# Transformer blocks on one core: first MLP products issued two tiles ahead, the last projection set between MLP steps, key loads set ahead of head saves

## The chip, the cores and the metric

The kernel runs on one core of a Trainium2 chip. The metric is the device time of one execution in microseconds; the kernel before has a median of 2254.26 us over 3 runs (2253.84 to 2258.37). Lower is better.

## The reference

```python
# x [8, 100, 512], ctx [8, 361, 512], float32
def L0(x):                       # 16 heads of width 128, keys extended by a bias row
    x = x + cross_attention(layer_norm(x), ctx, wq1, ..., bias_k1, bias_v1)
    x = x + cross_attention(layer_norm(x), ctx, wq2, ..., bias_k2, bias_v2)
    h = layer_norm(x)
    return x + gelu(h @ w_fc1 + b_fc1) @ w_fc2 + b_fc2          # 512 -> 2048 -> 512
def L1(x):                       # 16 heads of width 32
    q, k, v = layer_norm(x) @ q_w + q_b, ctx @ k_w + k_b, ctx @ v_w + v_b
    out = softmax(where(mask, q k^T / sqrt(32), min)) v
    x = x + out @ cproj_w + cproj_b
    y = gelu_tanh(layer_norm(x) @ fc_w + fc_b)
    return x + y @ proj_w + proj_b                              # 512 -> 2048 -> 512
out = L1(L0(x))
```

## The kernel before

**Layout.** Activations lie transposed: 128 features on the partitions, 400 rows (four batches of 100) along the free axis, in two halves; x is `xT[:, half, c]` with four chunks c of features. Every product of full precision is made of three matmuls on a high and a low part of each operand (`split_mms`), so one 128x512 weight tile against one half is 12 matmuls of 400 columns. The high part is a ScalarE copy with rounding, the low part a VectorE subtraction; for weights GpSimd makes both (`split`: L757 and L759).

**Order.** Nothing is scheduled at run time. Each engine has its own program with semaphore waits. Weight tiles come in one list, `JOBS`, sorted by a due step; SP loads them in that order into three stage buffers (`load_jobs(jobs_due(step) + 3)`), GpSimd splits them in that order into a ring of four slots (`mring`; a few go into `w1`), and a slot is free when the product that read the tile four places earlier has ended. SP's queue also carries context loads, saves and loads through DRAM, and issues strictly in its order: a wait in front of one item holds all behind it.

**Stages.** Two large attention blocks (up to step 256, not touched), MLP 0, the small attention, MLP 1. An MLP has 32 steps F, 16 for each half of the rows. `up(f)` multiplies weight tile ("a", f) with the normed input into a bank (bank f % 2); `gelu_high(f)` applies gelu into `gtmp` and rounds it into `part`; `gelu_low(f)` makes the low part; `down(f)` multiplies tile ("b", f) with the part tile into four accumulating banks `ACC`. TensorE runs `up(F+1)`, `down(F)` in step F. `up(16)` reads the norm of the second half. After 16 steps `mlp_add` adds the four banks to x on VectorE. `MLP_NORM` says in which step of an MLP a layer norm starts: norm 5 in step 0 and norm 6 in step 16 of MLP 0, norm 9 in step 0 of MLP 1. A norm started at step F takes sum at F+1, mean at F+2, centring and squares at F+3, their sum at F+4, variance at F+5, root and reciprocal at F+6, four scales on VectorE (L1548) and four high parts on ScalarE at F+7, four low parts on VectorE (L1495) at F+8. In each step VectorE does its gelu tile first.

**Between.** `queries1(0..3)` makes the queries of half 0 (query 0 in the last MLP step, in banks 0 and 1 by turns), SP saves them to DRAM (`save_q`) and loads them rearranged (`load_q`); then `keys1` in bank 0 and `values1` in banks 5, 6, 1 for the first batch. The high part of query Q >= 2 waits for the save of query Q - 2.

**Small attention.** 32 steps s of four units: logits (L1095), softmax, three transposes (L1106), `value_sums1` two steps behind. In each step SP saves the heads of step s - 3 (`save_heads`, L626, waits for the low part of the value sum), loads the keys of step s + 1 (`load_k`, L621, three issues), saves keys (L611), loads queries once in four steps (L605) and the heads back (`load_heads`, L636, four issues). `project1(0, c)` is done in step 19. At the end TensorE does the last two value sums, `up(32)` in step 32, `up(33)`, `up(34)`, then waits for the last heads, does `project1(1, c)` for the four c into banks 5, 6, 2, 3, and starts MLP 1 with `down(32)` behind the additions to x (L1505).

## Time and profile before

| | |
|---|---|
| median of 3 runs | 2254.26 us |
| profiled execution, its own time | 2260.57 us |
| its span, first to last instruction | 2258.8 us |
| mean granted TensorE clock | 0.987 |
| TensorE matmul busy | 2161.1 us (96%) |
| VectorE busy | 1605.4 us (71%) |
| ScalarE busy | 1183.9 us (52%) |
| GpSimd busy | 943.8 us (42%) |
| DMA, 16 engines | 52.5% on the hardware queue |

Busy is the time in which the engine executes an instruction; its idle time costs only where another engine waits for what comes late. The granted clock is 1 at 2.4 GHz; a stretch with a lower mean has spent a part of its time at 1.2 GHz. Times in rows count from the start of the span.

### The profile page before, as it was taken

To read this page: it belongs to the slowest core of one execution; us is meant where nothing else is said; L and a number is where in the kernel's file an instruction comes from. 1 tells how busy PE (TensorE), PEld (TensorE's weight loads), DVE (VectorE), ACT (ScalarE), POOL (GpSimd) and SP (SyncE) were. 2 spreads that over 40 slices of the span, in tenths; PEclk is the share of its full clock that TensorE was granted. 3 is DMA by queue.
4 is the path that set the end of the run, shared out by engine and by line. 5 is a ranking of instruction groups with operands and counts; after the bars stand their busy time and mean duration, and the time that the engine had idled before them with its cause. 6 is when DMAs were issued, how large, how long until landed. Compare 5 with 4: busy or idle time off the path is not lost.

```text
span 2258.8 us, 36858 instructions
## 1 busy us (share of the span) xinstructions
PE 2161.1 (96%) x12468; PEld 2099.6 (93%) x12468; DVE 1605.4 (71%) x3635; ACT 1183.9 (52%) x2838; POOL 943.8 (42%) x898
## 2 busy tenths in 40 slices
PE   6999999999999999999999999999999899998899
PEld 5999999999999999999999999998899778887899
DVE  6777688777778877777887777777466487788353
ACT  4555465555555555555555555565243376667232
POOL 4314444241444424234342424432788332232597
PEclk9999999999999999999999999999999999998999
DMA  4646455554645555464555546454543667765243
GB/s 136 140 87 142 102 121 101 120 128 83 151 101 113 102 125 122 85 148 105 110 110 116 126 83 151 109 102 83 139 125 103 167 189 199 206 199 160 84 132 108
DMA packets 162454, 283.08 MB, mean 125 GB/s; under 512 B 35424, under 2 KB 92896, under 8 KB 162272
## 3 DMA queue, kind: packets, MB, share of 16 engines
q1 hardware_dynamic: 162272, 280.73, 52.5%
q8 instruction: 105, 1.72, 0.3%
q14 instruction: 77, 0.63, 0.1%
HBM read 237.66 MB, written 29.88 MB: 118 GB/s over the span
## 4 chain that ended last, share of the span: by engine, by line
PE 80%; DVE 6%; DMA 4%; ACT 3%; POOL 3%; issue 2%; SPq 2%; POOLq 0%; DVEq 0%; ACTq 0%
PE bank L838 76%; PE bank L926 3%; POOL mring L759 1%; DMA ctxN_raw<-in_ctx 1%; POOL mring L757 1%; DVE ln_c L1548 1%; DVE hT L1495 1%; SPq L636 1%; DVE lnb L1541 1%; PE bank L1106 1%; ACT prob L1340 1%; DMA k<-k_parts 1%; DVE prob L1662 1%; POOL ln_c L813 1%; DMA y_parts<-qs 0%
## 5 line engine op out<-in xcount | busy, mean ns | idle before, releaser
L838 PE MATMUL bank<-ctxT,kring 128*128 128x362 f32 x3456 | 629.6, 330 | 4.4 <-DVE qs L1495 2.7
L757 POOL TENSOR_SCALAR mring<-stage 128x512 fp32r<-128x512 f32 x325 | 233.3, 718 | 899.2 <-PE bank L838 734.2
L838 PEld LDWEIGHTS bank<-ctxT,kring 128*128 128x128 f32 x3456 | 587.2, 190 | 7.6 <-issue 4.7
L838 PE MATMUL bank<-pT,ctxN 128*128 128x400 f32 (+1 forms) x2304 | 470.0, 351 | 0.6 <-DVE U L1499 0.3
L759 POOL TENSOR_TENSOR mring<-stage,mring 128x512 fp32r<-128x512 f32 x325 | 444.9, 1369 | 27.1
L838 PEld LDWEIGHTS bank<-pT,ctxN 128*128 128x128 f32 (+1 forms) x2304 | 407.1, 188 | 2.4 <-issue 1.2
L838 PE MATMUL bank<-hT,mring 128*128 128x400 f32 x1608 | 320.0, 348 | 13.8 <-DVE hT L1495 10.5
L838 PEld LDWEIGHTS bank<-hT,mring 128*128 128x128 f32 x1608 | 296.1, 190 | 18.3 <-issue 15.0
L838 PE MATMUL bank<-U,mring 128*128 128x400 f32 x1536 | 303.3, 348 | 8.1 <-issue 6.3
L838 PEld LDWEIGHTS bank<-U,mring 128*128 128x128 f32 x1536 | 275.3, 188 | 10.3 <-issue 7.9
L1234 ACT ACTIVATE kT<-bank,cols 128x361 fp32r<-128x361 f32 (+1 forms) x288 | 160.8, 558 | 211.8 <-PE bank L838 211.7
L1499 DVE TENSOR_TENSOR ctxN<-ctxN_raw,ctxN 128x384 fp32r<-128x384 f32 x256 | 189.2, 742 | 81.9 <-ACT ctxN L1234 81.9
L1234 ACT ACTIVATE U<-bank 128x400 fp32r<-128x400 f32 x256 | 127.8, 499 | 146.2 <-PE bank L838 144.3
L1499 DVE TENSOR_TENSOR U<-bank,U 128x400 fp32r<-128x400 f32 x256 | 146.2, 571 | 74.8 <-ACT U L1234 73.8
L1577 DVE TENSOR_SCALAR_CACHE_REDUCE prob<-bank 100x362 f32<-100x362 f32 x256 | 135.1, 528 | 88.1 <-PE bank L838 88.0
L1282 ACT ACTIVATE prob<-prob,stat 100x362 f32<-100x362 f32 x256 | 151.1, 590 | 74.7 <-DVE prob L1577 74.7
L1234 ACT ACTIVATE pT<-bank 128x300 fp32r<-128x300 f32 x384 | 160.0, 417 | 54.0 <-PE bank L926 37.6
L1499 DVE TENSOR_TENSOR pT<-bank,pT 128x300 fp32r<-128x300 f32 x384 | 175.6, 457 | 5.8 <-ACT pT L1234 5.8
L1234 ACT ACTIVATE ctxN<-ctxN_raw 128x384 fp32r<-128x384 f32 x256 | 131.7, 516 | 85.3 <-DMA ctxN_raw<-in_ctx 85.2
L838 PE MATMUL bank<-kT,qT 128*100 128x362 f32 x768 | 169.2, 328 | 4.2 <-DVE kT L1495 4.2
L1499 DVE TENSOR_TENSOR part<-gtmp,part 128x400 fp32r<-128x400 f32 x64 | 75.3, 1178 | 136.6 <-ACT part L1234 136.3
L1495 DVE SCALAR_TENSOR_TENSOR kT<-bank,cols,kT 128x361 fp32r<-128x361 f32 (+1 forms) x288 | 168.2, 584 | 4.6 <-ACT kT L1234 4.6
(103 smaller groups left out, 2942.1 us busy)
## 6 DMA issues: line engine op xcount, KB each, us to landing
ctxT_raw<-in_ctx SPq DMA_DIRECT2D x72, 724.0 KB, 7.5
ctxN_raw<-in_ctx SPq DMA_DIRECT2D x256, 192.0 KB, 3.6
k<-k_parts SPq DMA_DIRECT2D x96, 181.0 KB, 3.7
stage<-in_wk SPq DMA_DIRECT2D x64, 256.0 KB, 4.1
stage<-in_wq SPq DMA_DIRECT2D x64, 256.0 KB, 4.5
stage<-in_wv SPq DMA_DIRECT2D x64, 256.0 KB, 4.0
stage<-in_wo SPq DMA_DIRECT2D x64, 256.0 KB, 2.7
stage<-in_fa SPq DMA_DIRECT2D x64, 256.0 KB, 2.6
```

Of the source, the lines that this page charges most:

```text
L636: sp.dma_start(f32(attnT[r, :, a:a + LQ]), y_dram[t, r, :, i * LQ:(i + 1) * LQ]).then_inc(S.at_in, 16)
L757: nc.gpsimd.tensor_scalar(hi, src, 1.0, 1.0, ALU.mult, ALU.mult).then_inc(S.w_hi, 1)
L759: nc.gpsimd.tensor_tensor(lo, src, f32(hi), ALU.subtract).then_inc(S.w_ready, 1)
L813: nc.gpsimd.tensor_tensor(y, y, lnb[:, 1, :], ALU.mult).then_inc(S.ln_y, 1)
L838: mm = pe.matmul(dst, parts_l[a], parts_r[b], start=first and k == 0, stop=last and k == len(order) - 1)
L926: mm = pe.transpose(bank[T_BANK][:, t * LQ:(t + 1) * LQ], prob[0:LQ, n % PB, t * P:(t + 1) * P], ident[0:LQ, 0:LQ])
L1106: mm = pe.transpose(bank[T1_BANK[u % 2]][:, t * LQ:(t + 1) * LQ], prob1[0:LQ, u % PB, t * P:(t + 1) * P], ident[0:LQ, 0:LQ])
L1234: return nc.scalar.activation(dst, src, ACT.Identity, bias=bias)
L1282: nc.scalar.activation(x, x, ACT.Exp, scale=-1.0, bias=nmax[0:LQ, k:k + 1], accum_out=denom[0:LQ, k:k + 1]).then_inc(S.exp_ready, 1)
L1495: return nc.vector.scalar_tensor_tensor(out=dst, in0=src, scalar=bias, in1=f32(hi), op0=ALU.add, op1=ALU.subtract)
L1499: return nc.vector.tensor_tensor(dst, src, f32(hi), ALU.subtract)
L1577: nc.vector.tensor_scalar(prob[0:LQ, k, 0:LT], bank[2 + n % 2][0:LQ, 0:LT], -SCALE0, None, ALU.mult, ALU.min, accum_out=nmax[0:LQ, k:k + 1 ...
```

## The change

- `up(F + 2)` is issued in step F instead of `up(F + 1)`, on three banks (`UP_BANK`) with three part and gelu buffers (`MB = 3`). The list of tiles gives `a(f + 2)` ahead of `b(f)`.
- Query 0 is made in step 30 and query 1 in step 31 of MLP 0; the queries use banks 6, 0, 1, 6. `keys1(0)` waits for two queries instead of three, `values1(0, 1)` for four, `values1(0, 2)` for three.
- `up(32)` and `up(33)` are issued inside the attention's steps 32 and 33, behind the first third of a value sum. `project1(1, c)` is done behind `down` in steps 2 to 5 of MLP 1, all in bank 6, each waiting for the addition before; `down(32)` no longer waits for it.
- Norm 9 starts in step 5 of MLP 1 instead of step 0.
- In SP's loop `load_k` stands ahead of `save_heads`.

```diff
+MB = 3
-MLP_NORM = {0: {0: 5, 16: 6}, 1: {0: 9}}
+MLP_NORM = {0: {0: 5, 16: 6}, 1: {5: 9}}
...
         if f + 2 <= NF - 1:
-            add(T_MLP[0] + f - 1, "b", f)
-            add(T_MLP[0] + f, "a", f + 2)
-        else:
-            add(T_MLP[0] + f - 1, "b", f)
+            add(T_MLP[0] + f - 1, "a", f + 2)
+        add(T_MLP[0] + f - 1, "b", f)
     for j in range(4):
-        add(T_MLP[0] + NF - 1 + j // 2, "1q", j)
+        add(T_MLP[0] + NF - 2 + j // 2, "1q", j)
...
     for f in range(1, NF):
+        if f + 2 < NF:
+            add(T_MLP[1] + f - 1, "a", F + f + 2)
         add(T_MLP[1] + f - 1, "b", F + f)
-        if f + 2 < NF:
-            add(T_MLP[1] + f, "a", F + f + 2)
...
+        UP_BANK = [[0, 1, 6], [0, 1, 5]]
...
-        CPROJ_BANK = [[1, 1, 1, 1], [5, 6, 2, 3]]
+        CPROJ_BANK = [1, 6]
+        F_CPROJ = 2
...
         def q1_bank(Q):
-            return bank[Q % 2 if Q < 4 else X1_BANK][:, 0:ROWS]
+            return bank[[6, 0, 1, 6][Q] if Q < 4 else X1_BANK][:, 0:ROWS]
...
             for s in range(NS + BEHIND):                         # SP
+                if s + 1 < NS:
+                    load_k(s + 1)
                 if s >= BEHIND + 1:
                     save_heads(s - BEHIND - 1)
-                if s + 1 < NS:
-                    load_k(s + 1)
...
                 for F in range(NF):                              # TensorE
-                    if 1 <= F < NF - 1 and (m == 0 or F > 1):
-                        up(NF * m + F + 1)
-                    elif F == NF - 1 and m == 0:
-                        queries1(0)
+                    if F + 2 < NF:
+                        up(NF * m + F + 2)
+                    elif m == 0:
+                        queries1(F + 2 - NF)
                     down(NF * m + F)
+                    if m == 1 and F - F_CPROJ in range(DC):
+                        project1(1, F - F_CPROJ)
...
+                    if s >= NS and i == 0:
+                        up(NF + s - NS)
...
-                if s == NS:
-                    up(NF)
-            up(NF + 1)
-            up(NF + 2)
-            for c in range(DC):
-                project1(1, c)
             mlp_steps(1)
...
                 for F in range(NF):                              # VectorE; ScalarE alike
-                    if 1 <= F < NF - 1:
-                        gelu_low(NF * m + F + 1)
-                    elif F and m == 0:
-                        query1_low(0)
+                    if F + 2 < NF:
+                        gelu_low(NF * m + F + 2)
+                    elif m == 0:
+                        query1_low(F + 2 - NF)
+                    if m == 1 and F - F_CPROJ in range(DC):
+                        projected1(1, F - F_CPROJ)
```

## Rows read from the trace of the kernel before

**Rows 1.** Stretches: us; busy of PE, PEld, DVE, ACT, POOL; clock, DMA share, GB/s

```profile
1612.00:1765.00 153.00, 144.29 (x761) 140.82 (x762) 91.63 (x88) 56.37 (x95) 138.80 (x130) 0.98 0.43 131
1765.00:1793.00 28.00, 23.43 (x113) 20.90 (x111) 7.81 (x13) 6.48 (x10) 5.04 (x5) 0.94 0.73 178
...
2089.00:2118.00 29.00, 20.73 (x95) 19.74 (x95) 5.76 (x9) 4.63 (x7) 3.83 (x4) 0.86 0.23 77
2118.00:2256.00 138.00, 134.94 (x736) 133.02 (x735) 61.29 (x58) 41.49 (x71) 119.63 (x116) 1.00 0.37 112
```

**Rows 2.** Chain that ended last, merged: start us, us, what

```profile
2190.07 63.99 PE bank L838 x351
```

**Rows 3.** Timeline of TensorE, first MLP: start, us, line, count, idle before and releaser

```profile
1611.98 2.41 PE L838 MATMUL bank<-part,w 128*128 128x400 f32 x12 [0.76 <-DVE xT L1504]
...
1653.47 2.41 PE L838 MATMUL bank<-part,mring 128*128 128x400 f32 x12 [0.67 <-DVE part L1499]
...
1659.99 3.98 PE L838 MATMUL bank<-part,mring 128*128 128x400 f32 x12 [1.93 <-DVE part L1499]
...
1734.95 2.40 PE L838 MATMUL bank<-part,mring 128*128 128x400 f32 x12 [1.32 <-DVE part L1499]
...
1740.45 2.42 PE L838 MATMUL bank<-part,mring 128*128 128x400 f32 x12 [0.92 <-DVE part L1499]
```

**Rows 4.** Groups by line, 1612 to 1765: busy us, mean ns | idle before

```profile
L759 POOL TENSOR_TENSOR mring<-stage,mring 128x512 fp32r<-128x512 f32 x63 | 89.4, 1419 | 5.3
...
L757 POOL TENSOR_SCALAR mring<-stage 128x512 fp32r<-128x512 f32 x63 | 48.7, 773 | 14.4 <-PE bank L838 12.5 <-DMA stage<-in_fb 1.5
```

**Rows 5.** Timeline, from the MLP to the first logits

```profile
1768.30 9.32 SPq L594 DMA_DIRECT2D q_parts<-qs  x8
...
1775.04 3.11 PE L838 MATMUL bank<-ctxT,kring 128*128 128x362 f32 x12 [2.74 <-DVE qs L1495]
...
1775.43 0.59 ACT L1234 ACTIVATE qs<-bank,cols 128x400 fp32r<-128x400 f32 x1 [1.20 <-DMA q_parts<-qs]
...
1793.04 0.54 PE L1095 MATMUL bank<-k,q 96*100 96x362 f32 x1 [1.87 <-DMA k<-k_parts]
```

**Rows 6.** Waits of TensorE, 1793 to 2089: us, times, longest

```profile
PE bank L1095 <- DMA k<-k_parts: 9.2, 3, 4.5
...
PE bank L1095 <- issue: 2.2, 3, 1.2
```

**Rows 7.** Timelines of SP and of TensorE at the longest of these waits

```profile
2001.13 0.43 SPq L626 DMA_DIRECT2D y_parts<-qs  x1
...
2007.80 0.41 PE L1095 MATMUL bank<-k,q 96*100 96x362 f32 x1 [4.50 <-DMA k<-k_parts]
```

**Rows 8.** Timeline behind the small attention, into the second MLP

```profile
2089.01 2.87 PE L838 MATMUL bank<-hT,mring 128*128 128x400 f32 x12
...
2101.39 2.45 SPq L636 DMA_DIRECT2D qT<-y_parts  x4
...
2105.46 11.36 PE L838 MATMUL bank<-qT,w 128*128 128x400 f32 x48 [6.59 <-DMA qT<-y_parts]
...
2117.75 4.59 PE L838 MATMUL bank<-part,mring 128*128 128x400 f32 x24 [0.93 <-DVE xT L1505]
```

**Rows 9.** Timeline of the second MLP, steps 7 to 10

```profile
2145.31 2.35 PE L838 MATMUL bank<-hT,mring 128*128 128x400 f32 x12
...
2149.60 5.05 DVE L1548 SCALAR_TENSOR_TENSOR ln_c<-ln_c,cols,lnb 128x400 f32<-128x400 f32 x4
...
2156.90 5.05 DVE L1495 SCALAR_TENSOR_TENSOR hT<-ln_c,cols,hT 128x400 fp32r<-128x400 f32 x4
...
2157.13 2.40 PE L838 MATMUL bank<-part,mring 128*128 128x400 f32 x12 [0.74 <-DVE part L1499]
...
2162.99 2.42 PE L838 MATMUL bank<-part,mring 128*128 128x400 f32 x12 [1.28 <-ACT part L1234]
```

**Rows 10.** Timeline of VectorE inside the attention, GpSimd idle: the lows of norm 8

```profile
2077.96 1.17 DVE L1495 SCALAR_TENSOR_TENSOR hT<-ln_c,cols,hT 128x400 fp32r<-128x400 f32 x2
```

More of the change, by code:

```diff
@@ L1001, in up @@
                 for c in range(DC):
-                    mm = split_mms(bank[f % 2][:, 0:ROWS], w_cols(key, c), [hT_c(hT, 0, c), hT_c(hT, 1, c)],
+                    mm = split_mms(up_bank(f), w_cols(key, c), [hT_c(hT, 0, c), hT_c(hT, 1, c)],
                                    c == 0, c == DC - 1)
@@ L1019, in down @@
                 for c in range(DC):
-                    mm = split_mms(bank[ACC[c]][:, 0:ROWS], w_cols(key, c),
-                                   [part[f // NF][:, f % 2, p_, :] for p_ in range(2)],
+                    mm = split_mms(bank[ACC[c]][:, 0:ROWS], w_cols(key, c), gelu_parts(f),
                                    f % FF == 0, f % FF == FF - 1)
@@ L1133, in project1 @@
                         pe.wait_ge(S.q1_lo, 8)
[L1134 to L1135 removed]
+                    else:
+                        pe.wait_ge(S.y_lo, NS)
+                else:
+                    pe.wait_ge(S.c_add, DC * half + c)
                 for j in range(4):
[L1137 removed]
+                    mm = split_mms(bank[CPROJ_BANK[half]][:, 0:ROWS], w_cols(("1c", half, j), c),
                                    [attnT[:, p_, j * ROWS:(j + 1) * ROWS] for p_ in range(2)], j == 0, j == 3)
@@ L1185, in _ @@
             mlp_steps(0)
-            for Q in range(1, 4):
+            for Q in (2, 3):
                 queries1(Q)
@@ L1301, in gelu_high @@
                     act.wait_ge(S.a_mm, NS - 4)
-                if f >= 2:
-                    act.wait_ge(S.m_lo, f - 1)
-                    act.wait_ge(S.dn_mm, f - 1)
-                g = gtmp[f // NF][:, f % 2, :]
-                nc.scalar.activation(g, bank[f % 2][:, 0:ROWS], gelu, bias=col_c(bias, f % FF))\
+                if f % NF >= MB:
+                    act.wait_ge(S.m_lo, f - MB + 1)
+                    act.wait_ge(S.dn_mm, f - MB + 1)
+                g = gelu_out(f)
+                nc.scalar.activation(g, up_bank(f), gelu, bias=col_c(bias, f % FF))\
                     .then_inc(S.m_gelu, 1)
                 act.wait_ge(S.m_gelu, f + 1)
-                high(part[f // NF][:, f % 2, 0, :], g).then_inc(S.m_hi, 1)
+                high(gelu_parts(f)[0], g).then_inc(S.m_hi, 1)
             def query1_high(Q):
@@ L1438, in _ @@
             mlp_steps(0)
-            for Q in range(1, 4):
+            for Q in (2, 3):
                 query1_high(Q)
@@ L1698, in projected1 @@
                 dve.wait_ge(S.c_mm, DC * half + c + 1)
-                add_to_x(half, c, bank[CPROJ_BANK[half][c]][:, 0:ROWS], "L1_xattn_cproj_b").then_inc(S.c_add, 1)
+                add_to_x(half, c, bank[CPROJ_BANK[half]][:, 0:ROWS], "L1_xattn_cproj_b").then_inc(S.c_add, 1)
             def context_low(i, k):
@@ L1818, in _ @@
             mlp_steps(0)
-            for Q in range(1, 4):
+            for Q in (2, 3):
                 query1_low(Q)
@@ L1862, in _ @@
                     norm_low(8, (2 * (t - 10), 2 * (t - 10) + 1))
-                if s == NS:
-                    gelu_low(NF)
-            gelu_low(NF + 1)
-            for c in range(DC):
-                projected1(1, c)
+                if s >= NS:
+                    gelu_low(NF + s - NS)
             mlp_steps(1)
```

60 lines of the change are left out of this document (32 added, 28 removed).

## The prediction

> **What bounds the kernel now.** I read the busy time by stretch first [rows 1]. TensorE is the busiest engine in every stretch, and the change can only touch the last 650 us. Its idle time there is small and lies in known places: 8.7 us in the first MLP (153.00 - 144.29), 4.6 between MLP and attention, 8.3 of 29 behind the attention, 3.1 in the second MLP. The clock column shows where it also runs at the lower of its two levels, 1.2 instead of 2.4 GHz, for a part of the time: 0.94 ahead of the attention, 0.86 behind it. GpSimd, which splits each weight tile, is busy 138.80 of 153.00 us in the first MLP and 119.63 of 138.00 in the second. So TensorE sets the end, and GpSimd stands close behind it.
>
> Next, what one unit of work costs. The chain of waits has 351 matmuls in 63.99 us without a gap, 0.182 each, so a group of 12 (an `up`, a `down` or a `project1`) takes 2.19 us at the full clock [rows 2]. All sums below are in such groups.
>
> **First MLP.** TensorE's rows with a wait in front [rows 3] give the gaps of one kind: the VectorE half of a gelu tile comes late. 0.67 and 1.93 us behind norm 5, 1.32 and 0.92 behind norm 6. Behind the second, 12 matmuls took 3.98 us where the group behind the first took 2.41: the clock had fallen, 1.6 us more. The reader is to see that VectorE works off the four scales and four lows of a norm, some ten microseconds, around two gelu tiles. The change lets `up` run one step (two groups, 4.4 us) further ahead, with a third bank and a third part buffer, so between the end of `up(F)` and `down(F)` lie four groups, not two. All four gaps are shorter than the 4.4 us won, so I count them all as gone, with the clock they cost: 0.67 + 1.93 + 1.6 + 1.32 + 0.92 = 6.4. At the MLP's start `down(0)` waited 0.76 for the residual sum; `up(2)` now stands ahead of it and needs only an earlier sum: 0.8 more. The wait for x in front of `down(16)` stays: `mlp_add` still follows the end of `down(15)` on VectorE, behind one gelu tile and one weight tile, and one `up` covers 2.2 us of that, as before.
>
> What could take this back is GpSimd. It does a tile in 0.773 + 1.419 = 2.19 us on average [rows 4], as long as TensorE's group. Its 14.2 idle us of the stretch are partly given by TensorE's own gaps. Taking 7.2 out of the stretch leaves it 7.0, so the tiles still arrive, narrowly. Term: -7.2; bounds 0 (GpSimd takes over, every gap becomes a wait for a tile) and -7.2.
>
> **Between the MLP and the attention.** SP could start saving the queries only at 1768.30, behind a weight load that waits for the split of the last query tile, and that split waits for `down(31)`. The high part of query 2 waits for that save's landing, that of query 3 for the next one's, until 1775.43, and TensorE waited 2.74 for query 2's bank, until 1775.04; its next 12 matmuls took 3.1 us, partly at the lower clock [rows 5]. The change runs query 1 before `down(31)`: the split, and with it SP, comes one group (2.2 us) later against the work done, and query 3's low about 2.2 later. But `keys1(0)` now needs the banks of queries 0 and 1 only, and runs with `values1(0,0)` under the wait; what waits for query 3 is `values1(0,1)`. Behind query 2's low TensorE did one keys (3.1 us), two values and a second keys, and on that one hang the split, the save and the load of the keys, up to the first logits at 1793.04. Now the second keys hangs on query 3's low instead, with one values ahead of it; query 3's low ends at 1776.1 (high and low are 0.6 each), 1.1 behind 1775.04. So a keys and a values fall out of the chain, 3.1 and about 2.7 (12 x 0.182 x 512/400), and 1.1 comes in: 4.7 less; minus the 2.2 that SP starts later, minus some matmuls at the lower clock behind the wait: about -2. Bounds 0 and -4.6 (the stretch's whole idle time).
>
> **Keys first in SP's queue.** At each step `load_k` (three DMA issues) went behind `save_heads`, which waits for the value sum. Key loads came late three times, 9.2 us in all, 1.87 of it at the first logits; the two others make 7.3. Three more gaps in front of logits, 2.2 us, have no releaser shown [rows 6]. At the longest one, until 2007.80, SP came late out of its weight loads and issued the save (0.43 us) at 2001.13, then the keys [rows 7]; without the save in front they go half a microsecond earlier and are not behind its bytes. I take the small gaps for those at the first logits of a batch, where the query load stands behind `load_k`: with the keys issued during the wait for the value sum, it goes earlier by three issues, which at SP's 0.43 to 0.6 us for one covers them (1.2 the longest). What queues behind `load_k` now is `save_heads`; where the logits of the step before aren't done, it goes up to 1.5 us later, and ScalarE needs its landing only a step later. The Trainium skill (DMA: Bandwidth & Descriptors, Queues, rings and completion order) says that an engine takes descriptors in ring order; it speaks for the same direction and gives no price. I take -3: 2 for the small gaps, 1 for the two of half a microsecond. Bounds 0 and -9.5 (7.3 + 2.2).
>
> **Behind the attention.** The last heads come back by loads issued from 2101.39 to 2103.84, and TensorE stands 6.59 us until 2105.46 [rows 8]. Then the four `project1` take 11.36 us for 48 matmuls, where 48 x 0.182 is 8.7: 2.6 for the clock. `down(32)` waits 0.93 more. Lost in all: 10.1. In the new order TensorE has work between the end of `up(32)` (2091.9) and the heads, 13.6 us later: `up` 33 to 36 and `down` 32 to 34, seven groups of 2.19, are 15.3 us, and the last value sums come on top. The heads are there first. Against this: `up(32)` moves ahead of the second value sum, into a stretch at the lower clock (it took 2.87 there where 2.19 is full rate, and would take up to 4.0): 1.1, and it shifts the last head output by about 0.6, which is covered. And the tile of `down(34)` is loaded only behind the head loads in SP's queue, from 2103.8 on (0.6 later with the shift). With some 2.5 us to landing (between the 1.6 of the last head load and the 4.1 of the first) and 2.2 to split it is ready near 2109.4, where TensorE, behind its fifteen microseconds and the value sums, wants it at 2108 to 2109: I count 0.9. SP's order of the weight loads follows TensorE's new order. Term: -10.1 + 1.1 + 0.9 = -8.1. Bounds -5.5 (the clock falls all the same) and -10.1. The four additions to x lie on VectorE in steps that are a group longer than before.
>
> **Norm 9 in the second MLP: the new wait.** The norm of the second half moves from step 0 to step 5, since x is complete only after `project1`. Its low part then lies in step 13, and `up(48)`, which reads it, is issued in step 14; before, the low stood in step 8 and the product in step 15. [Rows 9] have the same sequence, five steps earlier: the `up` of the scaling step starts at 2145.31; the four scales end at 2154.65; ScalarE's high parts hold up the next gelu; the four lows run 2156.90 to 2161.95, 16.6 us after that start. TensorE reaches `up(48)` four groups after it, 8.7 us. So it waits 7.9 us, if VectorE's rows stay as long. They won't quite: with TensorE standing, GpSimd fills its four slots and stops, and the same low step took 1.17 for two, 0.59 each, when GpSimd was idle [rows 10], instead of 1.26. That takes 2.5 off: 5.4. I take 6.5. After such a wait the clock falls: 1.6 us were lost behind 1.93 of waiting [rows 3], 2.6 behind 6.59 [rows 8]; I take 2.0. What is given back is what norm 9 cost before, 0.74 and 1.28 [rows 9]. Term: +6.5 + 2.0 - 2.0 = +6.5. Bounds +3.4 (5.4, no fall) and +8.5 (7.9 and 2.6).
>
> The Trainium skill has a rule for each part. GPSIMD Engine Reference, Architecture: GpSimd's physical read and write port is shared with VectorE; the trace agrees (0.59 against 1.26), and by it the wait is nearer to 5.4. TensorE: Matmul & The Clock Gate, HAM oscillation, tells how an idle gap drops the clock and the work behind it is paid at half rate; it speaks against any new wait, so the sum would be nearer to +8.5.
>
> **Sum.** -7.2 - 2 - 3 - 8.1 + 6.5 = -13.8. The profiled execution took 2260.57 us (span 2258.8 and 1.8 around it) and goes to 2246.8. It lies 6.3 above the median of the three runs, 2254.26; I carry the difference over to that: 2240.5.
>
> **Rivals.**
> 1. GpSimd takes over in the first MLP (7.2 of gain gone): 2240.5 + 7.2 = 2247.7. For it: 2.19 against 2.19. Against: four slots of lead and 7.0 us left. Chance 0.14.
> 2. The new wait costs its upper bound and the keys gain nothing: 2240.5 + 2.0 + 3 = 2245.5. For it: a clock that fell after each gap. Chance 0.15.
> 3. The keys come early enough to empty both late loads and norm 9 meets an idle GpSimd: -9.5 instead of -3, +3.4 instead of +6.5: 2230.9. For it: the longest wait, 4.50, came right behind the save. Against: SP was late by more than the save. Chance 0.12.
> 4. No change that can be told: the upper bounds of norm 9, keys and the tail together with half of GpSimd's: 2240.5 + 2 + 3 + 2.6 + 3.6 = 2251.7. Chance 0.06.
> 5. Slower: after the wait at `up(48)` the clock stays at the lower level. 34 groups follow, each 2.19 us longer at 1.2 GHz. From 6.3 such groups on (13.8 / 2.19) the gain is gone, from 8.4 on it is slower by more than 0.2%; with 16, half of them, it is 2240.5 + 35.0 = 2275.5. Against it: the longest fall behind a wait that the rows show costs 2.6 us. Chance 0.05.
>
> The forecast itself keeps 0.48, with 2236 to 2245 as its own range. Two tenths of a per cent, 4.5 us, is about what a measurement of this kernel can tell from no change: 2249.8 and below is faster. That holds for the forecast, rivals 1 to 3 and a part of 4: 0.88; same 0.07, slower 0.05. The range 2232 to 2249 holds the forecast, rivals 1 and 2 and half of rival 3.
>
> **What would show it.** In the trace after: no wait of TensorE for a gelu part in the first MLP, and its stretch some 7 us shorter; no wait for the head loads, and no fall of the clock around it; one wait of 5 to 8 us in front of the 12 matmuls of `up(48)`, released by VectorE's low (hT, L1495 of before), with 3 to 5 us of matmuls longer than 2.35 behind it; waits on the key loads of 6 us instead of 7.3 and none of the small ones. I am wrong if GpSimd's tiles are named as releaser all through the MLPs, if `values1(0,1)` waits more than 3 us, or if the wait at `up(48)` is not there.

## The result

The changed kernel is slower by 0.6%. Beside four runs of the kernel before (median 2255.42 us, 2253.84 to 2258.37) four runs of it gave a median of 2269.42 us (2265.68 to 2274.33); the ratio is 1.0062, with a 95% interval of 1.0039 to 1.0084. The interval is clear of 1, so the sign is sure. I had forecast 2240.5, range 2232 to 2249. The profiled execution took 2274.33 us, span 2272.5, clock 0.983. Lines of the changed code stand 9 or 10 further down than those named above (`split_mms` is L848, logits L1105, `save_heads` L636, `load_heads` L646, `load_k` L631; L627 is the place in `load_k` where SP waits for the logits of the step two before, which free the key buffer).

### The profile page after: what moved, and what is told of

It is laid out like the page before. It is cut to its first block, busy times and chain, and to the rows that moved or that the text cites. A ratio compares the mean times of both kernels' runs of the same rounds, so it can differ in the third digit from the quotient of the medians.

```text
span 2272.5 us, 36855 instructions
## 1 busy us (share of the span) xinstructions
PE 2170.3 (96%) x12468; PEld 2106.2 (93%) x12468; DVE 1594.9 (70%) x3635; ACT 1182.5 (52%) x2838; POOL 943.1 (42%) x898
## 4 chain that ended last, share of the span: by engine, by line
PE 79%; DMA 6%; POOL 5%; DVE 3%; SPq 3%; ACT 2%; issue 2%; POOLq 0%; DVEq 0%; ACTq 0%
PE bank L848 74%; POOL mring L769 3%; PE bank L936 3%; DMA y_parts<-qs 3%; POOL mring L767 2%; SPq L646 2%; DMA ctxN_raw<-in_ctx 1%; SPq L631 1%; PE bank L1116 1%; DMA stage<-in_fb 1%; DVE hT L1504 1%; POOL ln_c L823 1%; PE bank L1105 0%; ACT prob L1350 0%; DVE ln_c L1557 0%
## 5 line engine op out<-in xcount | busy, mean ns | idle before, releaser
L848 PE MATMUL bank<-ctxT,kring 128*128 128x362 f32 x3456 | 630.3, 330 | 1.1 <-DVE ctxT L1508 1.1
L848 PEld LDWEIGHTS bank<-ctxT,kring 128*128 128x128 f32 x3456 | 588.7, 190 | 3.4 <-issue 1.4
L848 PE MATMUL bank<-pT,ctxN 128*128 128x400 f32 (+1 forms) x2304 | 471.1, 352 | 0.0
L848 PEld LDWEIGHTS bank<-pT,ctxN 128*128 128x128 f32 (+1 forms) x2304 | 408.7, 189 | 1.4 <-issue 0.2
L848 PE MATMUL bank<-hT,mring 128*128 128x400 f32 x1608 | 326.7, 353 | 24.9 <-DVE hT L1504 16.0
L848 PEld LDWEIGHTS bank<-hT,mring 128*128 128x128 f32 x1608 | 300.7, 193 | 31.3 <-issue 20.8
L848 PE MATMUL bank<-U,mring 128*128 128x400 f32 x1536 | 304.8, 349 | 8.1 <-issue 6.3
L848 PEld LDWEIGHTS bank<-U,mring 128*128 128x128 f32 x1536 | 276.9, 189 | 10.3 <-issue 7.9
L1244 ACT ACTIVATE pT<-bank 128x300 fp32r<-128x300 f32 x384 | 159.7, 416 | 57.3 <-PE bank L936 37.7
L848 PE MATMUL bank<-kT,qT 128*100 128x362 f32 x768 | 169.2, 328 | 4.2 <-DVE kT L1504 4.2
```

What stands on the lines that cost most here:

```text
L848: mm = pe.matmul(dst, parts_l[a], parts_r[b], start=first and k == 0, stop=last and k == len(order) - 1)
L1244: return nc.scalar.activation(dst, src, ACT.Identity, bias=bias)
```

## The profile after

Busy time by stretch, columns as in [rows 1], cut at the same points of the work:

```profile
1614.00:1768.00 154.00, 145.48 (x770) 140.37 (x769) 91.50 (x88) 56.26 (x95) 141.29 (x130) 0.99 0.43 130
1768.00:1797.40 29.40, 21.95 (x112) 19.20 (x111) 7.74 (x13) 6.33 (x10) 5.56 (x6) 0.95 0.68 168
1797.40:2095.00 297.60, 263.14 (x1479) 230.72 (x1480) 226.16 (x707) 198.38 (x525) 76.26 (x75) 0.95 0.65 186
2095.00:2130.00 35.00, 29.72 (x135) 28.54 (x134) 7.71 (x16) 10.02 (x20) 16.62 (x18) 0.81 0.40 121
2130.00:2270.00 140.00, 132.95 (x713) 131.37 (x712) 60.02 (x59) 38.04 (x65) 105.35 (x105) 0.98 0.35 104
```

No stretch is shorter by what I had promised. Measured from landmark to landmark (first matmul of a stage to first of the next, after minus before, one trace of each, us): up to the last product of the second large attention +2.6 (code that the change doesn't touch), first MLP +0.4, from the third query to the first logits +1.3, attention up to the last batch's value sums +6.8, the tail with the four `project1` -3.4, the second MLP +5.9. That is +13.6 of the 13.8 between the two spans.

**First MLP.** TensorE, rows with a wait in front, as in [rows 3]:

```profile
1678.77 2.46 PE L848 MATMUL bank<-hT,mring 128*128 128x400 f32 x12 [0.56 <-POOL mring L769]
1681.91 2.46 PE L848 MATMUL bank<-part,mring 128*128 128x400 f32 x12 [0.68 <-POOL mring L769]
...
1745.67 2.46 PE L848 MATMUL bank<-hT,mring 128*128 128x400 f32 x12 [0.95 <-POOL mring L769]
...
1760.22 3.95 PE L848 MATMUL bank<-hT,mring 128*128 128x400 f32 x12 [4.02 <-POOL mring L769]
```

The waits for a gelu part are gone; in their place stand waits with GpSimd as releaser, 7.1 us in five places. The longest is for the tile of query 0: in the list it stands behind two tiles, those of `down(30)` and `down(31)`, that TensorE now uses after it. GpSimd's two groups, as in [rows 4], show the same 63 tiles, with 18.2 us idle in front of them instead of 19.7:

```profile
L769 POOL TENSOR_TENSOR mring<-stage,mring 128x512 fp32r<-128x512 f32 x63 | 88.6, 1406 | 5.3
L767 POOL TENSOR_SCALAR mring<-stage 128x512 fp32r<-128x512 f32 x63 | 52.5, 833 | 12.9 <-PE bank L848 11.6 <-DMA stage<-in_fb 1.2
```

**Up to the first logits**, as in [rows 5]:

```profile
1781.26 3.04 PE L848 MATMUL bank<-w,ctxT 128*128 128x512 f32 x12 [1.09 <-DVE qs L1504]
...
1784.58 2.71 SPq L615 DMA_DIRECT2D q<-q_parts  x6
...
1787.34 0.90 SPq L621 DMA_DIRECT2D k_parts<-kT  x2
...
1792.93 2.69 SPq L631 DMA_DIRECT2D k<-k_parts  x6
...
1797.39 0.62 PE L1105 MATMUL bank<-k,q 96*100 96x362 f32 x1 [6.33 <-DMA k<-k_parts]
```

TensorE waits only 1.09 for the queries, as foreseen. But the first key save goes out at 1787.34, behind six query loads, though its low part had ended at 1781.70; 5.6 us after the issue it has landed and the key load may go. The gap moved from the wait for query 2 (2.74 in [rows 5]) to the first logits (1.87 there, 6.33 here).

**Attention.** SP's waits by releaser from 1800 to 2080 (us in total, times, longest), after and then before:

```profile
SPq L646 <- DMA y_parts<-qs: 60.2, 24, 4.0
SPq L627 <- PE bank L1105: 22.1, 11, 6.1
```

```profile
SPq L626 <- DVE qs L1495: 73.1, 23, 6.6
...
SPq L636 <- DMA y_parts<-qs: 7.0, 13, 1.9
```

Before, SP waited for VectorE (the low part of the value sum), that is, it was ahead of the work. After, it waits 24 times for the landing of a head save that it has itself just issued. For TensorE this means, in batches 4 and 5, waits of 1.62 and 5.53 us for key loads and one of 1.87 us for the heads of `project1(0)`; before, its waits for key loads there were 2.85 and 4.50, and it didn't wait for heads. One turn of its queue, after and before:

```profile
2037.73 1.47 SPq L631 DMA_DIRECT2D k<-k_parts  x3
2039.25 0.44 SPq L636 DMA_DIRECT2D y_parts<-qs  x1
2039.73 0.43 SPq L621 DMA_DIRECT2D k_parts<-kT  x1
2043.38 2.45 SPq L646 DMA_DIRECT2D qT<-y_parts  x4
2045.93 1.48 SPq L631 DMA_DIRECT2D k<-k_parts  x3
```

```profile
2033.35 0.34 SPq L626 DMA_DIRECT2D y_parts<-qs  x1
2033.79 1.40 SPq L621 DMA_DIRECT2D k<-k_parts  x3
2035.24 0.43 SPq L611 DMA_DIRECT2D k_parts<-kT  x1
2036.12 2.46 SPq L636 DMA_DIRECT2D qT<-y_parts  x4
...
2044.15 0.34 SPq L626 DMA_DIRECT2D y_parts<-qs  x1
```

Before, three key issues and a key save cover the landing; the turn is 5.2 us and SP idles until the next. After, 3.2 us of the landing are bare, the turn is 8.2 us, and it is followed by the next one at once.

**Tail and norm 9**, timeline as in [rows 8] and [rows 9]:

```profile
2097.04 4.20 PE L848 MATMUL bank<-hT,mring 128*128 128x400 f32 x12
...
2117.69 0.58 SPq L568 DMA_DIRECT2D stage<-in_fb  x1
...
2122.87 4.37 PE L848 MATMUL bank<-part,mring 128*128 128x400 f32 x12 [3.25 <-POOL mring L769]
...
2127.04 3.14 PE L848 MATMUL bank<-qT,w 128*128 128x400 f32 x12
...
2182.34 5.04 DVE L1557 SCALAR_TENSOR_TENSOR ln_c<-ln_c,cols,lnb 128x400 f32<-128x400 f32 x4
...
2189.61 2.27 DVE L1504 SCALAR_TENSOR_TENSOR hT<-ln_c,cols,hT 128x400 fp32r<-128x400 f32 x4
...
2192.02 4.34 PE L848 MATMUL bank<-hT,mring 128*128 128x400 f32 x12 [5.95 <-DVE hT L1504]
2196.16 2.74 PE L848 MATMUL bank<-part,mring 128*128 128x400 f32 x12
```

The wait for heads is gone. Tile b34, loaded behind the last heads at 2117.69, made TensorE wait 3.25 and the clock fell behind it. The new wait in front of `up(48)` is there: 5.95 us, then 2.4 us more for two groups (rows of 4.34 and 2.74, where neighbouring groups at the full clock have rows of 2.35 and 2.33, which overlap by 0.16).

## The experiments

Each run was timed in five rounds (e7 and e7b in three) beside the kernel before; the runs were made on four chips, so the ratios, each against the kernel before on the same chip, compare better than the medians where two runs come from different groups (e1, e2, e3, e6; e4, e7, e7b, e8; e9, e10, e11, e13; e14, e15, e16). Two stretches are read in all traces. A: from the start of the last 39 matmuls of the second attention block's projection to the end of query 3. B: from the first logits of a batch to those of the next, here for batches 4 and 5 (steps 16 to 23).

| kernel | median us | ratio to before | A | first logits wait | batch 4 | batch 5 |
|---|---|---|---|---|---|---|
| before | 2255.42 | 1 | 168.5 | 1.87 | 45.4 | 37.4 |
| after | 2269.42 | 1.0062 (1.0039 to 1.0084) | 168.9 | 6.33 | 49.3 | 44.2 |
| e1: after, heads first | 2259.51 | 1.0014 (1.0000 to 1.0028) | 167.5 | 6.47 | 44.1 | 38.4 |
| e2: before, keys first | 2269.39 | 1.0052 (1.0037 to 1.0067) | 163.5 | 2.22 | 49.8 | 44.6 |
| e3: e1, queries behind `down` | 2255.41 | 0.9995 (0.9984 to 1.0005) | 163.4 | 7.23 | 45.1 | 37.4 |
| e6: after, heads loaded later | 2273.15 | 1.0066 (1.0050 to 1.0081) | 168.4 | 7.05 | 50.0 | 40.4 |
| e8: after, both landings covered | 2268.62 | 1.0059 (1.0044 to 1.0074) | 169.3 | 7.59 | 49.3 | 39.9 |
| e14: after, heads loaded by GpSimd | 2259.72 | 1.0012 (0.9999 to 1.0025) | 167.9 | 6.99 | 45.3 | 37.3 |
| e16: after, weight loads spread | 2271.71 | 1.0062 (1.0049 to 1.0075) | 169.3 | 6.70 | 49.3 | 39.1 |
| e4: e3, norm 9 a step earlier | 2250.39 | 0.9980 (0.9968 to 0.9991) | 162.9 | 6.18 | 42.2 | 37.4 |
| e7: e1, light split | 2244.04 | 0.9945 (0.9929 to 0.9961) | 156.1 | 6.84 | 44.8 | 37.3 |
| e7b: before, light split | 2244.21 | 0.9945 (0.9929 to 0.9960) | 155.5 | 3.72 | 41.7 | 38.4 |
| e9: e4, norm 9 another step | 2247.87 | 0.9960 (0.9944 to 0.9976) | 162.9 | 7.42 | 44.7 | 38.1 |
| e10: e9, first keys ahead | 2242.42 | 0.9935 (0.9921 to 0.9950) | 163.6 | 0.84 | 44.2 | 37.5 |
| e11: e10, weight loads spread | 2237.24 | 0.9913 (0.9899 to 0.9927) | 165.9 | 1.92 | 42.6 | 33.1 |
| e13: e10, high parts on ScalarE | 2237.10 | 0.9910 (0.9896 to 0.9924) | 159.7 | 1.16 | 44.2 | 37.9 |
| e15: e11 and e13 | 2236.87 | 0.9903 (0.9887 to 0.9919) | 159.6 | 0.68 | 45.1 | 33.4 |

### Keys first

**e1, the order of before in SP's queue; e2, that one edit alone on the kernel before.**

```diff
-                if s + 1 < NS:
-                    load_k(s + 1)
                 if s >= BEHIND + 1:
                     save_heads(s - BEHIND - 1)
+                if s + 1 < NS:
+                    load_k(s + 1)
```

> The kernel after with one edit undone: in SP's loop save_heads stands ahead of load_k again. Theory A: with the keys first, the landing of each head save (about 3.3 us) is waited for with nothing issued meanwhile, so SP's turn (8.2 to 9 us) is longer than a step of the attention, and key loads and head loads come late. Then the stretch from the first logits to the turn goes back from 282.3 to about 275.5 us, the head loads at the end come some 2.7 us earlier, and the time is about 2259.5 us, 10 less than after. Theory B: the order is worth what I had priced (-3), and the attention's loss comes from elsewhere, from the phase in which the weight loads meet the key loads, or from up(32) and up(33) inside the last steps. Then the stretch keeps over 280 us and the time is 2270 to 2273.

> The kernel before with one edit of the change: load_k ahead of save_heads. Theory A: slower by 7 to 10 us (2262 to 2265), with SP at work back to back from the middle of the attention, its turn at 8 us or more, and no wait of SP for the low part of the value sums. Theory B, the term as I had predicted it: 2252, 3 less than before, bounds 0 and -9.5.

Theory A held in both, in e1 with its number; e2 cost more than its 7 to 10. e1 is 9.9 us below after (0.0048 in the ratios), e2 is 12.5 above the kernel before of its chip (2256.88). Batches 4 and 5 carry it: 93.5 and 94.5 us with the keys first (after, e2), 82.8 and 82.4 with the heads first (before, e1). My term of -3 was wrong in sign. Without it the rest of the change is worth nothing either (e1 1.0014).

**e6 and e8, keys first, with the landings covered by another order.**

```diff
                 if s + 1 < NS:
                     load_k(s + 1)
+                if s + AHEAD - 1 < NS:              # e8; in e6 the key save stays last
+                    save_k(s + AHEAD - 1)
+                if s >= BEHIND + 2:
+                    load_heads(s - BEHIND - 2)
                 if s >= BEHIND + 1:
                     save_heads(s - BEHIND - 1)
```

> The kernel after, keys first as there, but the heads of a step are loaded one step later, ahead of the next head save, so that no load stands right behind the save that it waits for. Theory A (the unhidden landing is the cost): SP's turn falls by about 3 us, from 8.2 to 9 to about 5.5, the attention's stretch goes from 282.3 to 276 or less; project1(0) in step 19 may wait for heads that come a step later, up to 4 us with its clock. Time 2260 to 2266. Theory B (the order of keys and heads itself, or bytes on the queues, is the cost): the stretch stays over 280 us and the time within 2 us of 2269.4.

> The kernel after with keys first, and SP's turn reordered: load_k(s+1), save_k(s+2), load_heads(s-4), save_heads(s-3). In e6 I had covered the landing of the head save and laid bare that of the key save (load_k followed 3.2 us behind its own save_k). Now each save has issues behind it for the length of its landing. Theory A: a turn is the sum of SP's issues (4.8 us) plus each landing that nothing covers; it falls from 8.2 to 9 to about 5.2, SP waits for the engines again, the stretch from first logits to the turn goes from 282.3 to 274 to 277, and the time to 2259 to 2263. Theory B: keys first costs by itself; the stretch stays over 280 and the time over 2267.

Theory A missed in both, and by its numbers e8 is theory B's (2268.62, the attention as long as in after). In e6 `load_k` stood right behind the key save that it reads, and SP waited for that landing instead, 12.5 us in nine turns: I had uncovered the other of the two landings. In e8 SP's issues of a turn take 4.9 us. In both SP waits for the work again; e6 and then e8, 1800 to 2080:

```profile
SPq L627 <- PE bank L1106: 90.5, 25, 11.7
```

```profile
SPq L627 <- PE bank L1106: 99.4, 26, 12.7
```

So SP was no longer full, and still nothing was won. Batch 5 went from 44.2 to 40.4 and 39.9, but batch 4 stayed at 50.0 and 49.3. The heads, loaded a step later, held `project1(0)` in step 19 for 3.12 and 3.08 us (1.87 in after), and new waits of 3.0 and 3.1 us stand in front of the first logits of batch 4, with no releaser shown. So neither is a clean test of the mechanism. Two readings were left: the landing wait in the queue, or the head save that stands behind `load_k`'s wait for free key buffers.

**e14, the head loads of steps 0 to 29 issued by GpSimd; e16, after with the loads of four weight tiles spread.**

```diff
-                if s >= BEHIND + 1:
+                if s - BEHIND - 1 >= 30:            # SP keeps the last two
                     load_heads(s - BEHIND - 1)
...
+            extra += [(T_ATT1 + t + BEHIND + 1.1, 4, heads_load, t) for t in range(30)]   # GpSimd
```

> The kernel after, keys first, and the head loads of steps 0 to 29 issued by GpSimd, not by SP; only the last two stay on SP. SP then never waits for the landing of a head save, and its turn is three key issues and two saves, about 2.8 us. Theory A (the keys cost because, with them first, nothing lies between a save and the load of the same heads in SP's queue, and all that follows stands behind that landing): batches 4 and 5 (steps 16 to 23) take 80 to 83 us from logits to logits, as in the kernels with heads first, not 93.5; the attention 285 to 290 us, not 296; the time 2258 to 2262. Theory B: with the keys first, load_k's own wait for free key buffers holds the head save (e8: 26 waits, 99 us), ScalarE's value sums and the heads come late whoever loads them; batches 4 and 5 stay over 88 us and the time over 2264.

> The kernel after, keys first, with one edit: the due steps of a32, a33, b32 and a34 spread over four steps, which in e11 took 5 us off the kernel with heads first (batch 5: 37.5 to 33.1 us). Theory A (SP is full: its turn of 8.2 us is as long as a step of TensorE): the spreading can't remove the debt, batches 4 and 5 stay at 88 us or more and after gains under 5 us. Theory B (the keys-first order only lengthens the one stretch in which SP comes late out of the weight loads): batches 4 and 5 fall to 80 or below, and the time to 2259 or below.

e14 decides between these two: 2259.72, the level of e1, with keys first and batches 4 and 5 at 82.6. SP's waits:

```profile
SPq L629 <- PE bank L1119: 136.3, 27, 11.0
```

The head save still stands behind `load_k`'s wait, longer than in e8, and it costs nothing that shows. From the first to the last logits the nine traces with heads first and the weight loads not spread take 284.3 to 290.6 us, the five with keys first and the heads loaded by SP (after, e2, e6, e8, e16) 295.9 to 302.4, and e14 287.1: the two groups don't meet. What costs, then, is the head load in SP's queue once the keys go first. e14 took the landing waits and the four issues (2.5 us) off SP together. The issues alone do no harm where the heads go first (before and e1 have them all, and SP waits for VectorE), and in after the bare landing is what makes the turn too long. But no run takes the landing alone away without a new wait, so its share by itself is argued, not measured. e14 and e1 are level, so keys first shows no gain once the harm is taken away, unless issuing on GpSimd hides one. e16 says little: batch 5 fell by 5.1 us (4.4 from e10 to e11), and theory A's bound for batches 4 and 5 (88) is met by 0.4; batches 2 and 6 came out 3.0 and 2.6 longer in its trace, and the time didn't fall.

### The first MLP

**e3, on e1: the queries behind `down` in the last two steps, in the order of the list of tiles.**

```diff
                     if F + 2 < NF:
                         up(NF * m + F + 2)
-                    elif m == 0:
-                        queries1(F + 2 - NF)
                     down(NF * m + F)
+                    if F + 2 >= NF and m == 0:
+                        queries1(F + 2 - NF)
```

> The kernel of e1 (heads first), and in the last two steps of MLP 0 TensorE does down(F) ahead of the query, as the list of tiles has them. Theory A: the wait of 4.02 us for the tile of query 0 and the clock's fall behind it (1.6 us) are there because that tile is split fourth behind a and b tiles while TensorE asks for it third; in the list's order both go, and the time is 5.6 us below that of e1. Theory B: GpSimd is late here in any order (it had idled under 1 us in the four steps ahead), so the wait only moves to down(30) or down(31), and the time is within 1.5 us of e1's.

4.1 us below e1, stretch A 4.1 shorter: between the two theories. The wait for query 0's tile fell from 4.00 to 1.87, without a fall of the clock behind it: part order, part GpSimd's rate.

```profile
1758.50 2.48 PE L848 MATMUL bank<-hT,mring 128*128 128x400 f32 x12 [1.87 <-POOL mring L769]
```

The six traces with the queries ahead and a full split (after, e1, e6, e8, e14, e16) have A at 167.5 to 169.3, the five with `down` ahead and GpSimd's full split (e3, e4, e9, e10, e11) at 162.9 to 165.9; e11 is the longest because in its trace the clock fell behind the same wait of 1.87.

**e7 on e1, e7b on the kernel before: a light split.** Both leave out three quarters of the low parts of MLP 0's weights and of the first queries.

```diff
+                if key not in IN_W1 and (key[0] in ("a", "b") and key[1] < NF or key[0] == "1q"):
+                    lo, src, hi = lo[:, 0:D // 4], src[:, 0:D // 4], hi[:, 0:D // 4]
                 nc.gpsimd.tensor_tensor(lo, src, f32(hi), ALU.subtract).then_inc(S.w_ready, 1)
```

> The kernel of e1, and in MLP 0 GpSimd makes the low part of a weight tile on 128 of its 512 columns only (the other columns of the low part hold older values: this leaves out three quarters of the low parts of MLP 0's weights and of the first queries, so the output isn't the reference's). GpSimd's 2.19 us for a tile fall to about 1.2. Theory A: GpSimd's rate is what took the place of the gelu waits; the seven waits for tiles (8.8 us, 1.6 for the clock behind the longest) go, the stretch from down(0) to the third query falls from 161.5 to 151 us or below. Theory B: the tiles come late because of the slots of mring and the order of the list; then the longest wait, for query 0's tile, keeps over 2 us and the stretch stays over 156.

> The kernel before with the same edit: the low part of MLP 0's weight tiles on 128 of 512 columns only (three quarters of them left out, the output isn't the reference's). It is the measure for e7: what one tile ahead costs when GpSimd is no limit. Theory A: the waits for gelu parts (4.8 us, 1.6 for the clock) stay for the larger part, since VectorE's norm work around them stays, and are some tenths shorter each as it meets GpSimd less often: the stretch goes from 161.1 to 155 to 158 us, 4 to 7 above e7's. Theory B: GpSimd's share of VectorE's time made these waits too; then they fall under 1 us in all and the stretch equals e7's within 1.5 us, so that two tiles ahead is worth nothing in either case.

For e7 theory A held: no wait for a tile is left, A is 156.1, or 148.7 in the measure of the expectation (less 7.4 for the 39 matmuls). For e7b theory B did: no wait for a gelu part is left and with one tile ahead A is 155.5. So two tiles ahead show no gain with a fast GpSimd. With the full split they show none either: A is 162.9 to 165.9 at best, and 168.5 and 163.5 in the two traces with one tile ahead (before, e2). The gelu lows on VectorE say why; before, and e7b:

```profile
L1499 DVE TENSOR_TENSOR part<-gtmp,part 128x400 fp32r<-128x400 f32 x30 | 34.2, 1142 | 54.8 <-ACT part L1234 54.6
```

```profile
L1501 DVE TENSOR_TENSOR part<-gtmp,part 128x400 fp32r<-128x400 f32 x30 | 17.7, 591 | 75.2 <-ACT part L1236 75.2
```

The same instruction takes 1142 ns beside GpSimd's full split and 591 beside the light one. The gelu parts came late in [rows 3] because of GpSimd's work (e7b changes nothing else), and lookahead turned that debt into late tiles. The Trainium skill (GPSIMD Engine Reference, 1. Specifications) names this case: the interface to SBUF is shared with VectorE and contended by VectorE's instructions with two SBUF inputs. The trace agrees (1142 against 591 ns); gelu part and buffer are two.

**e13, on e10: ScalarE makes the high part of 96 weight tiles of the two MLPs.** The steps in which it works on a norm are left out.

```diff
+            def tile_high(key):                      # ScalarE
+                j = JOB[key]
+                act.wait_ge(S.w_in[j % STAGE], 16 * (j // STAGE + 1))
+                act.wait_ge(*released(IN_M[M_AT[key] - MS]))
+                high(place_of(key)[0], stage[:, j % STAGE, :]).then_inc(S.wa_hi, 1)
...
+                    # step F: tile_high of b(F + 1) ahead of gelu(F + 2), of a(F + 4) behind it
```

> The kernel of e10, and in both MLPs ScalarE makes the high part of most weight tiles (a copy with rounding, as for the value and key weights), GpSimd only the low part: 1.42 instead of 2.19 us for a tile. Skipped in the steps in which ScalarE has a norm's squares, root or high parts. Theory A (from e7 and e7b: GpSimd's time for a tile is what bounds MLP 0, as tiles that come late, and through VectorE's gelu lows, 1.03 to 1.15 us each beside 0.59 with a light split): the waits for tiles in MLP 0 fall from 4 to 8 us to under 2, the stretch by 5 to 8 us, the time 5 to 10 below e10. Theory B: ScalarE's copies, about 0.65 us each and two in a step of 4.4 us, come in front of the gelu of the next tile, and the gelu parts become late instead: no faster than e10, waits named by ScalarE's part.

5.3 us below e10; the waits for tiles fell to one of 1.19, the gelu lows to 824 ns:

```profile
L783 POOL TENSOR_TENSOR mring<-stage,mring 128x512 fp32r<-128x512 f32 x64 | 90.4, 1421 | 36.5 <-ACT mring L1258 31.3 <-PE bank L862 3.4
...
L1532 DVE TENSOR_TENSOR part<-gtmp,part 128x400 fp32r<-128x400 f32 x30 | 24.6, 824 | 55.4 <-ACT part L1258 55.3
```

The time is at the low end of theory A; stretch A is 3.9 shorter, less than its 5 to 8, and GpSimd still makes 19 of the 64 high parts there.

### Norm 9, the first keys, the weight loads

**e4, on e3: project1 and norm 9 one step earlier. e9: norm 9 another step, and b34 loaded ahead of the last heads.**

```diff
-MLP_NORM = {0: {0: 5, 16: 6}, 1: {5: 9}}
+MLP_NORM = {0: {0: 5, 16: 6}, 1: {3: 9}}          # e4: {4: 9}
-        F_CPROJ = 2
+        F_CPROJ = 1
...
             save_heads(NS - 1)
+            load_jobs(JOB[("b", NF + 2)] + 1)         # e9 only
             load_heads(NS - 1)
```

> The kernel of e3 (heads first in SP's queue, queries behind down), with project1(1, c) in steps 1 to 4 of MLP 1 and norm 9 from step 4, each one step earlier than in the change. Theory A: the wait in front of up(48), 5.95 us in the kernel after, is only the distance in groups between the norm's scales and up(48); one step is two groups, 4.4 us, so 1.5 us are left and the fall of the clock behind it (2 of 4.3 us for 12 matmuls) goes: 5.5 to 6.5 us below e3, about 2249. Theory B: with TensorE at work GpSimd stays busy, VectorE's lows take 1.26 instead of 0.57 us each and the norm comes as late as before by its own length: the wait stays over 3.5 us and the time is less than 2.5 below e3.

> The kernel of e4 with norm 9 started in step 3, so that its sum follows the last addition within step 4, another step earlier; and SP loads tile b34 between the last head save and the last head load, while it would only wait for the landing. Theory A (the wait at up(48) is distance alone, with VectorE's lows at their long 1.25 us): of e4's 4.05 us nothing is left, nor of the 2.0 and 0.9 us for the clock behind it, 6.5 us in all; b34 had no wait in e4's profile but 2.98 us with 2.0 of clock in e3's, so its part is 0 to 5. About 2244, 6 below e4. Theory B: the norm's own operations push the gelu parts of those steps back (VectorE is the bound there), and less than 3 us of the 6.5 come out.

e4's median is 5.0 us below e3's (3.4 by the ratios), but it kept a wait of 4.05, and theory B was right about why:

```profile
2159.72 4.99 DVE L1504 SCALAR_TENSOR_TENSOR hT<-ln_c,cols,hT 128x400 fp32r<-128x400 f32 x4
```

Its lows took 1.25 us each, where they had taken 0.57 while TensorE stood and GpSimd with it: 4.4 us won, 2.7 given back by the longer lows. The clock behind the wait cost no less than in after (rows of 4.34 and 3.23 us). In e9 `up(48)` doesn't wait at all. 2.5 us came of it by the medians, 4.5 by the ratios, since the heads now came 2.67 us late for `project1(1, 0)`; e9 mixes two edits, and which of them made that wait isn't shown.

**e10, on e9: the first keys ahead of the query loads. e11, on e10: four due steps instead of one.**

```diff
-            load_q(0)
-            load_q(1)
             save_k(0)
-            save_k(1)
+            load_q(0)
             load_k(0)
+            save_k(1)
+            load_q(1)
```

```diff
-    for t in (("a", F), ("a", F + 1), ("b", F), ("a", F + 2)):
-        add(T_ATT1 + 20, *t)
+    for i, t in enumerate((("a", F), ("a", F + 1), ("b", F), ("a", F + 2))):
+        add(T_ATT1 + 20 + i, *t)                      # e11
```

> The kernel of e9, and ahead of the attention SP's queue reads save_k(0), load_q(0), load_k(0), save_k(1), load_q(1), where it read load_q(0), load_q(1), save_k(0), save_k(1), load_k(0). Theory A: the first logits wait (6.18 us in e4, 6.33 in the kernel after) because the first key save stands behind six query loads that wait for the last query save, so that its landing starts 6 us late; the wait goes below 1 us and the time 5 to 6 us below e9. Theory B: what the first logits wait for is the queries' own way through memory; their load can't start before the last query save has landed, about 4 us behind the end of its issue, and the wait keeps over 3 us.

> The kernel of e10 with the due steps of tiles a32, a33, b32 and a34 spread over four steps of the attention instead of one, so that SP doesn't stand behind three weight loads in one turn (6.0 us in the kernel before, right ahead of the longest wait for keys, 4.5 us). Theory A: that wait falls by most of its length, 3 to 4 us below e10. Theory B: those loads wait for GpSimd's splits, and these for slots that project1(0) sets free; spread out they hold SP in several turns by less, and the sum stays the same within 1.5 us.

Theory A in both. In e10 the key save goes out at 1775.92, behind the queries' saves alone, and the first logits wait 0.84:

```profile
1775.92 0.55 SPq L621 DMA_DIRECT2D k_parts<-kT  x1
1778.86 1.29 SPq L615 DMA_DIRECT2D q<-q_parts  x3
1780.25 1.33 SPq L631 DMA_DIRECT2D k<-k_parts  x3
```

In e11 the longest wait for keys (4.64 us in e10) is gone, and batch 5 takes 33.1 us, where all kernels with heads first before it had 37.3 to 38.4; the time fell by 5.2, more than theory A's 3 to 4.

**e15, both together.**

> e11 and e13 together: weight loads spread, and high parts of weight tiles on ScalarE. If the two gains lie in different stretches (5.2 us in the attention, 5.3 in the MLPs, both below e10's 2242.4) they add up: about 2232. If the one only uncovers the other's wait, 2236 or more.

2236.87, ratio 0.9903 (0.9887 to 0.9919): not told apart from e11 or e13. The full sum of the two gains would be a ratio of about 0.9888, just inside the interval, so that they don't add is likely and not shown. A is short (159.6) and batch 5 too (33.4), but in its one trace the attention from first to last logits took 287.9 us, against 278.7 in e11. Kernels with the same attention code differ there by up to 6 us from trace to trace (284.3 in e4, 290.6 in e3), and what makes that stays open. All three beat both kernels.

## Why the prediction was wrong

**Keys first, -3: the step that failed, by sign and most of all by size.** I wrote that what queues behind `load_k`, `save_heads`, "goes up to 1.5 us later, and ScalarE needs its landing only a step later". I asked who waits for the save on ScalarE, and did not ask what stands next in SP's own queue: `load_heads`, which waits for the landing of that same save. In the old order the key issues had covered it. The row for it, 13 waits of 7.0 us in all against 73.1 us of waiting for VectorE, was one view away. Measured: +6.8 in the attention of the two traces, 9.9 (e1 against after) and 12.5 (e2 against before) in the medians. No rival let the keys cost anything: I had put the term's bounds at 0 and -9.5 and so excluded a loss without giving a reason.

**First MLP, -7.2: wrong, rival 1 was right, and for a reason beyond it.** I had compared 2.19 with 2.19 and held four slots of lead for enough. The gaps became waits for tiles, and e7b shows that the gaps themselves were made by GpSimd. One more thing was read too firmly: stretch A of the kernel before is 168.5 in the trace of [rows 3], but 163.5 in e2, whose first MLP is the same code; there the two waits behind norm 5 are 0.17 and 1.28 and the clock doesn't fall:

```profile
1656.49 2.40 PE L838 MATMUL bank<-part,mring 128*128 128x400 f32 x12 [0.17 <-DVE part L1499]
...
1662.35 2.42 PE L838 MATMUL bank<-part,mring 128*128 128x400 f32 x12 [1.28 <-ACT part L1234]
```

Of the 6.4 us that I counted, 2.7 were missing in that second execution; another 1.6 of the difference is a fall of the clock behind the wait for x at `down(16)`, which I hadn't counted. Against 163.5, after's 168.9 is a loss of 5.4. Most of that loss is an order that can be read in the diff: query 0 overtakes two tiles in TensorE's program and not in the list (4.1 us in e3). I had not laid the two side by side.

**Between MLP and attention, -2: measured +1.3.** The wait for the queries fell as I had it. I had the second keys at the end of the chain; it was SP's order, six query loads ahead of the first key save (with that order changed e10 is 5.5 us below e9).

**Behind the attention, -8.1: measured -3.4.** The mechanism was right, the heads are covered; the mis-sized term is tile b34. I had counted 0.9 for it; it cost 3.25 and some 2.8 for the clock (rows of 4.37 and 3.14, where 2.35 and 2.33 are full rate). What decides this wait stays open. It is 0.48 in e1, with the heads first, but 2.98 and 3.04 in e3 and e7, with the heads first too, and there is none over 0.5 in e16, with the keys first: SP's debt alone doesn't make it. `up(32)` at half rate cost 1.3 more than the 2.87 of before, 1.1 counted.

**Norm 9, +6.5: right.** 5.95 of wait and 2.4 for the clock, less 2.0 given back, is 6.4, and the second MLP is 5.9 longer; I had 6.5 and 2.0 for the first two. VectorE's lows ran at 0.57 with GpSimd idle, as [rows 10] had it. (Four lows at 0.59 instead of 1.26 take 2.7 off, not the 2.5 of my sum; and the forecast with rivals 1 to 3 has a chance of 0.89, not 0.88.) The clock came back within two groups, so rival 5, the slow side, had the wrong mechanism: the kernel is slower without it, and that its 2275.5 lies nearest to the measured time is chance.

**Sum.** Of the 27.5 us between the forecast for the profiled execution, 2246.8, and its 2274.33, 9.8 are the keys' term inside the attention, 7.6 the first MLP, 4.7 the tail, 3.3 the queries' stretch, 2.6 the untouched part, and norm 9 gave 0.6 back.

## What to carry to other kernels

In an in-order queue, a load that waits for a save holds up all behind it unless other issues lie between the two for as long as the landing takes; when an item is moved, look at each wait behind it in the same queue, not only at the engines, and at who needs the moved item next (in e6 and e8 it was `project1(0)`). Before looking ahead further on one engine, ask whether the late operand is late because another engine slows it: here lookahead moved such a debt and didn't pay it. And read a gap in a second execution before counting it as gain.

## What the runs showed that I had not expected

- A landing is long here: from issue to landing the 400 KB head save has a median of 4.2 us in the kernel after (2.9 in e8), the 362 KB key save 4.7, each key load 3.3. The Trainium skill (DMA: Bandwidth & Descriptors, Anatomy of one DMA — SWDGE (gpsimd) path) puts the fixed part at about 2 us for a DMA that GpSimd issues, mostly the receipt of the write; these are issued by SP, and no run here splits them.
- VectorE's 128x400 subtraction from two SBUF inputs: 591 ns with a light split on GpSimd, 824 with GpSimd making 64 low and only 19 high parts, 1142 with it making both for 63 tiles.
- What a wait costs in clock behind it varies from execution to execution more than with its length. Behind the waits of 1.87 for query 0's tile nothing was lost in e3, e4, e9 and e10, and 1.5 us in e11. The two groups behind waits of 4.0 us in front of a product took 1.3 to 2.8 us more than at the full clock (seven traces), those behind waits of 5.8 to 6.0 us 1.7 to 2.4 (eight traces). The keys' six matmuls behind the first logits took 2.0 us instead of 1.16 behind the wait of 6.33 in the kernel after, and also behind the one of 1.87 in the kernel before; behind 1.92 and 2.22 (e11, e2) they took 1.16.
